# Attention probabilities: high halves transposed as float16 by TensorE, low halves by one DMA a head

## The reference

```python
q = heads(hidden_states @ W_q); k_t = heads(text_ehs @ W_k); v_t = heads(text_ehs @ W_v)
probs_t = softmax(einsum("bhsd,bhtd->bhst", q, k_t) * Dh ** -0.5)
text_out = einsum("bhst,bhtd->bhsd", probs_t, v_t)
attn_scores = einsum("bhsd,bhnd->bhsn", q, k_ip) * Dh ** -0.5
qsem = l2norm(einsum("bhst,bte->bhse", probs_t, text_ehs))
sem = einsum("bhse,bne->bhsn", qsem, l2norm(ip_ehs))
probs_ip = softmax(attn_scores + 0.5 * sem) * spatial_mask[None, None, :, None]
ip_out = einsum("bhsn,bhnd->bhsd", probs_ip, v_ip)
out = (text_out + ip_out) @ W_out + b_out + residual
```

## Time and profile before

| | |
|---|---|
| median of three runs | 787.72 us |
| the profiled execution | 787.76 us, of which its span is 786.0 us |
| PE busy | 752.7 us, 96% |
| DVE busy | 661.3 us, 84% |
| ACT busy | 583.6 us, 74% |
| POOL busy | 445.5 us, 57% |
| the chain that ended last | PE 91% |

### The profile page before, as it was taken

The page is one execution under the profiler, slowest core; times in us unless marked ns, Lnnn a source line. Parts: engine busy times, 40 slices in busy tenths (PEclk is TensorE's granted clock), DMA queues, the critical chain, the costliest instruction groups (busy, mean ns, idle before and its releaser), DMA issues.

```text
span 786.0 us, 23801 instructions
## 1 busy us (share of the span) xinstructions
PE 752.7 (96%) x7730; PEld 589.2 (75%) x7730; DVE 661.3 (84%) x1960; ACT 583.6 (74%) x1702; POOL 445.5 (57%) x558
## 2 busy tenths in 40 slices
PE   5899999999999999999999999999999999999983
PEld 3568778787877878787787878778787777878661
DVE  4878898988989898898989889898998989889883
ACT  4378787877878787787878778787877878777770
POOL 4035574656647465664746566474656647464762
PEclk8999999999999999999999999999999999999996
DMA  8313222221412223140222314022231402021000
GB/s 268 100 50 74 73 68 61 61 79 43 104 27 67 63 58 81 42 107 24 68 65 57 83 41 107 21 70 65 54 87 38 109 22 69 19 52 42 9 2 15
DMA packets 71465, 50.02 MB, mean 64 GB/s; under 512 B 16640, under 2 KB 71280, under 8 KB 71344
## 3 DMA queue, kind: packets, MB, share of 16 engines
q1 hardware_dynamic: 67648, 44.66, 21.9%
q10 hardware_dynamic: 3696, 3.84, 1.7%
HBM read 20.80 MB, written 2.38 MB: 29 GB/s over the span
## 4 chain that ended last, share of the span: by engine, by line
PE 91%; issue 2%; DVE 2%; POOL 2%; DMA 1%; ACT 1%; ACTq 0%; SPq 0%; POOLq 0%; DVEq 0%
PE ps_prep L475 22%; PE ps_gram L574 19%; PE ps_pT L556 13%; PE ps_gram L575 12%; PE ps_score L548 6%; PE ps_prep L530 5%; PE ps_val L582 2%; PE ps_val L584 2%; PE ps_prep L527 1%; PE ps_prep L505 1%; PE ps_prep L610 1%; PE ps_prep L507 1%; DMA xt_sb<-in_x_t 1%; POOL dual L407 1%; POOL nrm L417 1%
## 5 line engine op out<-in xcount | busy, mean ns | idle before, releaser
L407 POOL TENSOR_TENSOR dual<-prob 112x371 f32<-112x371 f32 x320 | 282.9, 884 | 302.4 <-ACT prob L753 283.2
L574 PE MATMUL ps_gram<-gram_hi,pT_hi 125*128 125x371 f16 (+1 forms) x960 | 303.9, 320 | 0.0
L575 PE MATMUL ps_gram<-gram_lo,pT_hi 125*128 125x371 f16 (+2 forms) x960 | 255.9, 267 | 0.0
L747 ACT ACTIVATE pT_hi<-ps_pT 125x336 f16<-125x336 f32 x320 | 144.6, 452 | 143.4 <-PE ps_pT L556 139.9
L737 ACT ACTIVATE prob<-ps_score,low 112x371 f32<-112x371 f32 x320 | 184.0, 575 | 16.3 <-DVE low L912 9.8
L912 DVE TENSOR_REDUCE low<-ps_score 112x1 f32<-112x371 f32 x320 | 171.3, 535 | 28.5 <-PE ps_score L548 24.8
L917 DVE TENSOR_TENSOR pT_lo<-ps_pT,pT_hi 125x336 f16<-125x336 f32 x320 | 160.0, 500 | 38.2 <-ACT pT_hi L747 34.0
L927 DVE CUSTOM_DVE_ANT_0 quad_junk<-ps_gram,dual 112x371 f32<-112x371 f32 x320 | 171.1, 535 | 12.4 <-PE ps_gram L575 6.0
L753 ACT ACTIVATE prob<-prob 112x371 f16<-112x371 f32 x320 | 168.9, 528 | 0.0
L582 PE MATMUL ps_val<-val,pT_hi 125*128 125x42 f16 (+1 forms) x960 | 166.8, 182 | 0.0
L556 PE MATMUL ps_pT<-ident,prob 112*125 112x112 f32 x960 | 156.9, 272 | 5.6 <-DVE pT_lo L917 3.7
(11 more groups left out here) (183 smaller groups left out, 1405.8 us busy)
## 6 DMA issues: line engine op xcount, KB each, us to landing
ctx_sb<-in_ctx_t SPq DMA_DIRECT2D x15, 750.0 KB, 4.5
k_st<-k_lo SPq DMA_DIRECT2D x62, 70.3 KB, 2.1
k_st<-k_hi SPq DMA_DIRECT2D x60, 70.3 KB, 2.1
q_st<-q_hi SPq DMA_DIRECT2D x64, 48.0 KB, 2.0
k_st<-k_lo SPq DMA_DIRECT2D x62, 46.9 KB, 2.0
q_st<-q_lo SPq DMA_DIRECT2D x60, 48.0 KB, 2.0
k_st<-k_hi SPq DMA_DIRECT2D x60, 46.9 KB, 2.0
x_sb<-in_x SPq DMA_DIRECT2D x16, 140.0 KB, 2.4
```

Of the source, the lines that this page charges most:

```text
L407: nc.gpsimd.tensor_tensor(dual[:, h % 2, :], prob[:, h % 4, 0:TX], prob_16[:, h % 2, :], ALU.subtract).then_inc(s_dual, 1)
L574: nc.tensor.matmul(ps_gram[h % 2][:, 0:TX], hi, gh[0:TROWS[i], i, :], start=(i == 0), stop=False, skip_group_check=True)
L575: last = nc.tensor.matmul(ps_gram[h % 2][:, i * TC:TX], hi, gl[0:TROWS[i], i, i * TC:TX], start=False, stop=(i == NT - 1), skip_group_chec ...
```

## The change

- The probabilities are rounded to float16 by ACT first (`prob_hi`, four slots), and PE transposes that copy, as float16, into the bank read as float16. ACT still copies it out (`turned_out`).
- POOL makes the low halves in the untransposed form (`prob_lo`, four slots), and SP issues one transposing DMA a head from them to `pT_lo` (`turn_lo`).
- DVE no longer reads the transposed bank; it makes `dual` = 2 x probabilities - high half (`duals`), and the factor in `norms` changes with it.
- PE multiplies with the values two heads later (`VAL_LATER`), when the DMA has landed; ACT's `half_out` follows at h = 11 and h = 1.
- The token blocks are 128, 128 and 115 rows instead of 125, 125 and 121.
- SP's list is interleaved with the heads: a transposing DMA first in each, then at h = 0 the loads, at h = 2 to 9 two copies of Q, at h = 8 to 15 two copies of K, at h = 17 the residual rows. The 20 small `vip_diag` loads are spread over the first two batches.
- Half of the norms and inverse roots are done ahead in every batch, as before only in the last.

```diff
-TC = T // 3
+TC = P
-VALS_STEP, POW_STEPS, EXP_STEP = 0, (3, 4, 5, 6), 9
+HI_SLOTS = LO_SLOTS = 4
+VAL_LATER = 2
+AHEAD_VALS_STEP, AHEAD_NORM_STEPS, AHEAD_POW_STEPS = 13, (14, 15, 16, 17), (18, 19)
+VALS_STEP, POW_STEPS, EXP_STEP = 2, (5, 6), 9
+Q_STACK_STEP, K_STACK_STEP, LOAD_X_STEP = 2, 8, 17
...
+            def turn_lo(b, h):
+                g = H * b.n + h
+                sp.wait_ge(s_prob_lo, g + 1)
+                reached(sp, s_val, g + 1 - LO_SLOTS)
+                sp.dma_start_transpose(pT_lo[:, h % LO_SLOTS, :, 0:S], prob_lo[:, h % LO_SLOTS, :]).then_inc(s_pT_lo[h % LO_SLOTS], 16)
...
             def body(b, prepare, turning, finishing):
-                if turning:
-                    load_ctx(b.next().next())
-                    load_xt(b.next().next())
...
-                if prepare:
-                    stack_q(b.next())
-                    stack_k(b.next())
-                    load_x(b.next())
+                for h in range(H):
+                    if h + 2 < H:
+                        turn_lo(b, h + 2)
+                    elif prepare:
+                        turn_lo(b.next(), h + 2 - H)
+                    if turning and h == 0:
+                        load_ctx(b.next().next())
+                        load_xt(b.next().next())
...
+                    if prepare and 0 <= h - Q_STACK_STEP < 8:
+                        stack_q(b.next(), part=slice(2 * (h - Q_STACK_STEP), 2 * (h - Q_STACK_STEP) + 2))
+                    if prepare and 0 <= h - K_STACK_STEP < 8:
+                        stack_k(b.next(), part=slice(2 * (h - K_STACK_STEP), 2 * (h - K_STACK_STEP) + 2))
+                    if prepare and h == LOAD_X_STEP:
+                        load_x(b.next())
...
-            def duals(b, h):
+            def probs_lo(b, h):
                 g = H * b.n + h
-                pool.wait_ge(s_prob_16, g + 1)
-                reached(pool, s_quad, g - 1)
-                nc.gpsimd.tensor_tensor(dual[:, h % 2, :], prob[:, h % 4, 0:TX], prob_16[:, h % 2, :], ALU.subtract).then_inc(s_dual, 1)
+                pool.wait_ge(s_prob_hi, g + 1)
+                reached(pool, s_pT_lo[h % LO_SLOTS], 16 * (g // LO_SLOTS))
+                nc.gpsimd.tensor_tensor(prob_lo[:, h % LO_SLOTS, 0:TX], prob[:, h % 4, 0:TX], prob_hi[:, h % HI_SLOTS, 0:TX],
+                                        ALU.subtract).then_inc(s_prob_lo, 1)
...
             def transposes(b, h):
                 g = H * b.n + h
-                pe.wait_ge(s_prob, g + 1)
-                reached(pe, s_pT_lo, g)
+                turned = ps_pT[:, :].bitcast(F16)[:, 0:NT * S]
+                pe.wait_ge(s_prob_hi, g + 1)
+                reached(pe, s_pT_hi, g)
                 for i in range(NT):
-                    last = nc.tensor.transpose(ps_pT[0:TC, i * S:(i + 1) * S], prob[:, h % 4, i * TC:(i + 1) * TC],
-                                               ident[0:S, 0:S])
+                    last = nc.tensor.transpose(turned[:, i * S:(i + 1) * S], prob_hi[:, h % HI_SLOTS, i * TC:(i + 1) * TC],
+                                               ident_16[0:S, 0:S])
...
+            def values_ready(b, h):
+                g = H * b.n + h
+                pe.wait_ge(s_pT_lo[h % LO_SLOTS], 16 * (g // LO_SLOTS + 1))
...
+                    gram_part(b, h, 0)
+                    values_ready(*late)
+                    for i in range(NT):
+                        val_part(*late, i)
+                        if i + 1 < NT:
+                            gram_part(b, h, i + 1)
...
+            def turned_out(b, h):
+                g = H * b.n + h
+                act.wait_ge(s_pT, g + 1)
+                reached(act, s_val, g + 1 - HI_SLOTS)
+                turned = ps_pT[:, :].bitcast(F16)[:, 0:NT * S]
+                nc.scalar.activation(pT_hi[:, h % HI_SLOTS, :, 0:S], turned.rearrange("p (c s) -> p c s", s=S), ACT.Copy).then_inc(s_pT_hi, 1)
             def probs_hi(b, h):
...
+                nc.scalar.activation(prob_hi[:, h % HI_SLOTS, 0:TX], prob[:, h % 4, 0:TX], ACT.Copy).then_inc(s_prob_hi, 1)
...
                 for h in range(H):
                     if h + 1 < H:
-                        probs_hi(b, h + 1)
+                        turned_out(b, h + 1)
...
-                    if h + 1 < H:
-                        halve(b, h + 1)
+                    if h + 2 < H:
+                        probs_hi(b, h + 2)
...
-                nc.vector.tensor_tensor(pT_lo[:, h % 2, :, 0:S], ps_pT[0:TC, 0:NT * S].rearrange("p (c s) -> p c s", s=S),
-                                        pT_hi[:, h % 2, :, 0:S], ALU.subtract).then_inc(s_pT_lo, 1)
+                nc.vector.scalar_tensor_tensor(out=dual[:, h % 2, :], in0=prob[:, h % 4, 0:TX], scalar=2.0, in1=prob_hi[:, h % HI_SLOTS, 0:TX],
+                                               op0=ALU.mult, op1=ALU.subtract).then_inc(s_dual, 1)
```

More of the change, by code:

```diff
@@ L160, in build @@
         prob = sb("prob", [S, 4, T])
-        pT_hi = sb("pT_hi", [TC, 2, NT, S_PAD], F16)
-        pT_lo = sb("pT_lo", [TC, 2, NT, S_PAD], F16)
-        prob_16 = sb("prob_16", [S, 2, TX], F16)
+        prob_hi = sb("prob_hi", [S, HI_SLOTS, T_PAD], F16)
+        prob_lo = sb("prob_lo", [S, LO_SLOTS, T_PAD], F16)
+        pT_hi = sb("pT_hi", [TC, HI_SLOTS, NT, S_PAD], F16)
+        pT_lo = sb("pT_lo", [TC, LO_SLOTS, NT, S_PAD], F16)
         dual = sb("dual", [S, 2, TX])
@@ L292, in spread_v_ip, with stack_q, stack_k @@
-            def spread_v_ip():
+            def stack_q(a, terms=range(4), part=slice(0, 16)):
+                if part.start == 0:
+                    reached(sp, s_score, H * (a.n - 1))
+                    sp.wait_ge(s_prep_lo, NM * a.n + place(a, PIECE_Q) + 1)
+                for dst, src in q_restack(a.odd, terms)[part]:
+                    sp.dma_start(dst, src).then_inc(s_qst[a.odd], 16)
+            def stack_k(a, terms=range(4), part=slice(0, 16)):
+                if part.start == 0:
+                    sp.wait_ge(s_prep_lo, NM * a.n + place(a, PIECES_K[-1]) + 1)
+                    sp.wait_ge(s_kip, a.n + 1)
+                for dst, src in k_restack(a.odd, terms)[part]:
+                    sp.dma_start(dst, src).then_inc(s_kst[a.odd], 16)
@@ L367, in _ @@
             nc.gpsimd.memset(attn[:, C:CC * P], 0.0)
-            nc.gpsimd.memset(prob[:, :, TX:T], 0.0)
+            nc.gpsimd.memset(prob_hi[:, :, TX:T_PAD], 0.0)
+            nc.gpsimd.memset(prob_lo[:, :, TX:T_PAD], 0.0)
             for v in val:
@@ L461, in tail @@
                 for step in range(TEXT_OUT_STEP + 1):
-                    end(b.last(), step, ahead=True)
+                    end(b.last(), step)
             all_batches(body, tail)
@@ L596, in products, with late_values @@
                     for i in range(NT):
-                        gram_part(i)
-                        val_part(i)
+                        val_part(*late, i)
+                        if i + 1 < NT:
+                            gram_part(b, h, i + 1)
+            def late_values(b, h):
+                values_ready(b, h)
+                for i in range(NT):
+                    val_part(b, h, i)
             def finish(f, k, made):
@@ L675, in tail @@
             def tail(b):
+                for h in range(H - VAL_LATER, H):
+                    late_values(b.last(), h)
                 for k in range(NF):
@@ L806, in _ @@
             exps(start, 1)
+            probs_hi(start, 0)
             make_hi(start, PIECES_V[2], SETUP_BANKS)
-            probs_hi(start, 0)
-            halve(start, 0)
+            probs_hi(start, 1)
+            turned_out(start, 0)
             exps(start, 2)
@@ L962, in soft @@
                         reached(dve, s_text_out, f.n)
-                    last = norms(f, k, HH if ahead else 0, H)
+                    last = norms(f, k, HH, H)
                 elif k == 4:
-                    dve.wait_ge(s_rn, len(POW_STEPS) * (f.n + 1))
+                    dve.wait_ge(s_rn, POWS * (f.n + 1))
                     reached(dve, s_fin_exp, f.n)
@@ L1107, in body @@
                         split_lo(b.next().next(), SPLIT_STEP[h])
[L1108 removed]
+                    if h in AHEAD_NORM_STEPS:
                         norms_ahead(b, AHEAD_NORM_STEPS.index(h))
@@ L1112, in tail @@
                 for k in range(SOFT):
-                    soft(b.last(), k, ahead=True)
+                    soft(b.last(), k)
                 for k in range(NF):
```

159 lines of the change are left out of this document (81 added, 78 removed).

## The result

The changed kernel takes 1069.26 us (median of 4 runs, 1068.06 to 1071.69), the kernel before 787.48 on the same chip: a ratio of 1.358 [1.356, 1.361] (in brackets, here and below, the 95% interval). I had forecast 868, with a range of 805 to 940. The direction was right and the two large waits, for the context and for K, stood where the prediction put them; the size was off by 201 us.

The account below looks back on a forecast made before the run. PE's own work was taken to bound fifteen of sixteen batches, its saving lost in waiting for ACT. 787.8 + 25 + 2 (loop) + 21 (context) + 32 (K) = 868 us, range 805 to 940.

Parts of the forecast that it names:

- PE's saving: PE's transposes as float16 with 112 columns: 0.17 us less a head, 54 us, 56 with the block size.
- The loop: ACT waits each head for the 0.47 us trip of prob_hi to PE and back: +25 us, +2 in the last batch.
- the term of 27: Cost of ACT and PE waiting for each other each head, on top of 787.8; alone it would give 815.
- In a batch ACT is busy 35.96: ACT's side of the loop: 35.0 of this plus 20 trips of 0.47, 44.4 us if ACT led in every head.
- The context: Context load queued on SP behind transposing DMAs lands late for ACT's split in head 2: 1.5 us in 14 batches, +21 us.
- K: Last K copies stand on SP behind head 17's transposing DMA; PE's next scores wait 2.1 us in 15 batches, +32 us.
- I take 0.64: Time a transposing DMA occupies SP, taken from a plain copy; bounds 0.37 and 1.3 us.
- heads 11 to 14 make up: SP, 1.5 us late after four copies in each of heads 8 and 9, catches up before the last K copies.
- rival A: Transposing DMA occupies SP longer: 913 us at 1.0 us each, about 935 and more at 1.5; over 900, chance 0.16.
- The clock still 1.00: Sign of a right forecast: PE's granted clock stays 1.00, with PE busy near 42 of 51 us a batch.
- Hidden low halves: The low halves' path through POOL and DMA to pT_lo lands before the value products in head h+2 need it: 0 us.
- DVE's dual at no cost: DVE's SBUF instruction replacing its PSUM subtraction: 0.05 us more a head, covered by 5.9 idle; bound +15 us without cover.

Follow-up runs that it names:

- e13: Changed kernel with earlier context, prob_hi a head earlier, one transposing DMA per two heads, ten low-half slots, K copies first, fexp and first output step later: 816.8 us.
- e4: Changed kernel with ACT rounding the probabilities (prob_hi) one head earlier: 1001.2 us, 68 us less.
- e1: Changed kernel with a plain copy of the same size in place of each transposing DMA, low halves left untransposed: 951.1 us, 118 us less.
- e3: Changed kernel with the 16 copies of K issued from ACT's queue instead of SP's: 913.4 us, 156 us less.
- e6: Changed kernel with earlier context loads, K copies from ACT, prob_hi a head earlier (859.5 us), and POOL's low-half subtraction cut from 371 to 32 columns: 843.8 us.
- e14: e13 with POOL's subtraction of the low halves cut to 32 columns, the rest left zero: 791.4 us.

## Why the prediction was right and where it was wrong

**PE's saving: right.** The three transposes start 0.05 us apart, and what follows them starts 0.16 after the first, taken 0.14; PE's own work comes to 42.9 us a batch in e13, and heads 3 to 10 are there 0.17 shorter than before, as forecast. The Trainium skill's 275 ns for one ("TensorE: Matmul & The Clock Gate", Part 4: PE-mode transpose) would by my estimate, three in a row, have made it 0.8 us a head. As the length of one it is near the trace (224 ns in the mean), but three overlap: 0.31 to 0.32 us from the start of the first to the end of the third.

**The loop: the mechanism right, the sum some 20 us too small.** The trip is 0.41, taken 0.47; a head without extras in the last batch takes 1.79, taken 1.87. Outside heads 2, 3, 16 and 17 a batch is 1.4 us above the forecast, 21 us in 15 batches beside the term of 27. The step that failed here is "In a batch ACT is busy 35.96", taken as all that ACT needs: ACT also waits for DVE, 0.44 us in head 8 and 1.1 at `fexp` in head 10 (in 14 of the batches; in the kernel before it waited there only in the last), and the loop puts both on the path. The 68 us of e4 are no measure of this term. The 27 stand on top of the time before, so they already contain the 56 us that PE would have saved: by my own sums undoing the loop was to give up to 83. It gave 68, of which 45 are the context's.

**The context: place right, 21 us forecast, 51 measured.** In the batch shown ACT waits 2.86 instead of 1.5. SP starts the load 4.39 us after T(1), by my count 3.36: 0.6 since the transposing DMA ahead of it costs 1.25 from start to start and not 0.64, and 0.4 since POOL came to `prob_lo` later, from a small step of the norms (`nrm`). And ACT wants it 0.3 earlier, since heads 0 and 1 took 2.59 and 2.64, not 2.88 and 2.72 (for head 0 I had read the distance of the scores, 3.05; the transposes of the kernel before stand 2.82 apart). Head 3 behind it was slow as well, 3.1 to 3.8 us for 2.2 in six of the eight batches from the third on; that is the lower clock behind the stall, which was not in the sum.

**K: the step that failed.** "I take 0.64, the nearest row, another SBUF to SBUF transfer." It is 1.20, and the run with a copy of 0.62 in its place (e1) prices the step at 118 of the 201 us. A head with two copies then needs 2.58 us of SP, and the heads with four 3.86, where heads 8 to 15 last 2.6 on average. So SP no longer makes up what the heads with four copies cost, as the prediction had it ("heads 11 to 14 make up"): it is 5.2 us late at head 12 and still 6.1 at head 17, where e1 has 1.4 and 0.2. The wait is 8.2 instead of 2.1. The upper bound, twice a copy or 1.3, did hold it, and rival A names the mechanism, but its times (913 at 1.0 us, 935 and more at 1.5) are too low too: they let the wait at K grow by 2.7 for 0.36, where it grew by 6.1 for 0.56.

**The half clock was left out.** "The clock still 1.00" was in the list of what would show the forecast right; it is 0.89. A stall of 8 us costs itself and then the next head: 3.9 us instead of the 2.5 of e3, 15 times, some 20 us.

**By intervals**, in the batch of 64.43, the 13.2 us above the forecast are 7.2 in head 16 and 1.6 in head 17 (K and the clock), 1.6 and 1.4 in heads 2 and 3 (the context and the clock), and 1.4 in all others, near the 1.5 that ACT waits for DVE in heads 8 and 10. Times 15 that is 198 of the 201 us.

**Hidden low halves: nearly right.** The DMA lands in 2.3 us, but PE does wait for it (27.9 us in 35), since SP issues it late. **DVE's dual at no cost: wrong**, and mostly hidden as long as larger waits stood ahead of it: 16 us in e6, 25 in e14.

Of the two places of the Trainium skill that I set against each other, "Advanced Engine Details and Errata" (X-Bar Transpose) has such DMAs as fast as regular ones, and the trace agrees for the landing: 2.3 us against 2.2 for the plain copy. For the issue it disagrees, 1.20 against 0.62. "VectorE: DVE Perf Modes" (The three transpose paths) gives its 1309 ns for one block without saying of what; my estimate of 3.9 us for three does not hold, since three blocks land in 2.3 us and six occupy SP no longer than two. The price that decided is one of the issuing queue, and neither place states it.

## What to carry to other kernels

Before a DMA of a new kind goes onto a queue that also carries what others wait for, take its occupancy of the queue as the open number, and sum the queue's list over the whole batch against the intervals: past the point where it no longer catches up, each 0.1 us counts once per head, not once (here 0.59 more per DMA made SP 5.9 us later at head 17). If the price is one per DMA, put more into each. Where a change closes a loop between two engines, every wait of either inside the loop is on the path from then on, so an engine's busy time is too little for its side of the sum. And when a single edit gives more than its term, look in which heads it gives it, before the term is called too small: in e4 most of the gain was another wait's.

## What the runs showed of the hardware

The DMA that transposes occupies its queue 1.19 us with two blocks of 128 columns, 1.20 with three and 1.23 with six (medians of 320, 320 and 160); a plain copy of the same halves 0.62.

DVE's instruction with two operands in SBUF takes 0.53 us alone and longer while GpSimd works. Of its 320 in the changed kernel the 129 with no work of POOL beside them take 0.541 us at most; the 149 with more than 0.3 us of it beside them have a median of 0.87. DVE, then POOL, of the changed kernel:

```profile
204.58 0.53 DVE L978 SCALAR_TENSOR_TENSOR dual<-prob,prob_hi 112x371 f32<-112x371 f32 x1
...
211.01 1.45 DVE L978 SCALAR_TENSOR_TENSOR dual<-prob,prob_hi 112x371 f32<-112x371 f32 x1
```

```profile
210.36 0.84 POOL L441 TENSOR_TENSOR prob_lo<-prob,prob_hi 112x371 f16<-112x371 f32 x1 [0.78 <-ACT prob_hi L809]
211.15 0.91 POOL L432 TENSOR_TENSOR text_lo<-ctx_sb,text_hi 128x375 f16<-128x375 f32 x1
```

The first has no work of POOL beside it. The second is stretched by 0.92 us, and POOL works beside it for 1.05 us (211.01 to 212.06). DVE's instructions with one operand in PSUM keep their length beside POOL: `quad_junk` takes at most 0.548 us in all its 320, and `pT_lo` of the kernel before at most 0.509. The kernel before took its low halves from PSUM on DVE and made `dual` on GpSimd, so it had none of this. The Trainium skill has the rule ("SBUF — State Buffer", SBUF: two separate sides): a DVE instruction with two SBUF inputs and a GpSimd instruction that reads SBUF exclude each other, and the one that comes second "fully blocks". The trace agrees, and I had not looked for it. My sum gave `dual` 0.05 us more than the subtraction before it, which took 0.50 in the mean; it takes 0.69.
